# Linear attention merged with the third feed-forward part: another order of the steps inside a pass

## The reference, cut to what matters

```
x = x + _L2_xattn_ref(_layernorm(x, axis=-1), ctx_4096, ctx_4096)
x = x + _L2_ffn_ref(_layernorm(x, axis=-1), L2_ffn_router_w, L2_ffn_A, L2_ffn_B)
x = x + _L3_xattn_ref(_layernorm(x, axis=-1), ...)
```

## The kernel before

| step | engine, line | pass t works on |
|---|---|---|
| y transpose (y_tr) | PE L923, psY | t-3 |
| kv product | PE L913, psSO<-arena,kT | t-1 |
| e transpose (e_tr) | PE L929 | t |
| LN5 transpose, LN6 transpose | PE L614, psQ (or psTP) | t-4; e-2 |
| gate product | PE L628, psSO<-wkv,hT | e |
| out product | PE L951 to L953, psTP | t-2 |
| hidden transpose | PE L856 | e |
| expert product | PE L869, psKV | e |
| x add | DVE L1898 | t-3 |
| kvs | DVE L1901, L1904 (k_sb) | t-1 |
| statistics | DVE L1537 to L1539 | t-3 |
| eT low half | DVE L1515 kT | t |
| gates | DVE L1611 to L1572, with one exponential on ACT, L1142 | e |
| y | DVE L1917, L1919 (prob) | t-2 |
| LN5, LN6 low half (`ln_lo`) | DVE L1515 hT | t-4; e-2 |
| hidden low half | DVE L1515 oT | e |
| expert add | DVE L1838 | e-1 |
| maximum for k's softmax (ctx_max) | DVE L1878 | t+2 |
| q exponential, q copy (q_hi) | ACT L1394, L1108 qT | t-1 |
| ln_hi | ACT L1108 hT | t-4; e-2 |
| normalisation (`ln_norm_act`) | ACT L1373, xn | t-3; e-1 |
| kvs_lo, q_lo, rstd, nmr | POOL L573, L580, L451, L563 | |

## Time and profile before

### The profile page before, as it was taken

One profiled execution on the slowest core, in us unless ns is written; L12 is line 12 of the kernel. 1 busy time (PEld: TensorE's weight loads), 2 busy tenths in 40 slices (PEclk: granted clock), 3 DMA queues, 4 the chain that ended last, 5 costly groups with the idle time before them and its releaser, 6 DMA issues.

```text
span 1657.8 us, 27915 instructions
## 1 busy us (share of the span) xinstructions
PE 1544.3 (93%) x9690; PEld 1345.1 (81%) x9690; DVE 1064.4 (64%) x2585; ACT 820.7 (50%) x2869; POOL 336.9 (20%) x353
## 2 busy tenths in 40 slices
PE   6999999999999989889999999999999997767988
PEld 5898999999999978778888888888888776655766
DVE  6566556655655687756666666666666876754664
ACT  4556445554545553355555555555555414425540
POOL 4102101110101021222222223122222213313110
PEclk9999999999999999999999999999999997868989
DMA  5101010100001001101010101010100001100001
GB/s 199 31 26 57 9 51 27 39 27 26 26 27 39 27 28 48 39 26 39 26 39 26 39 26 43 22 64 24 42 30 4 30 4 51 61 1 20 33 4 51
DMA packets 13710, 59.43 MB, mean 36 GB/s; under 512 B 2131, under 2 KB 3155, under 8 KB 8454
## 3 DMA queue, kind: packets, MB, share of 16 engines
q1 hardware_dynamic: 13574, 57.67, 9.9%
HBM read 55.57 MB, written 2.10 MB: 35 GB/s over the span
## 4 chain that ended last, share of the span: by engine, by line
PE 51%; issue 29%; DVE 11%; POOL 4%; ACT 3%; DMA 1%; POOLq 0%; SPq 0%; ACTq 0%; DVEq 0%
PE psY L772 12%; PE psQ L697 8%; PE psKV L717 7%; PE psSO L760 2%; PE psSO L666 2%; PE psQ L682 2%; POOL wo L438 2%; PE psQ L1044 1%; PE psTP L682 1%; DVE wq L1515 1%; PE psSO L667 1%; PE psTP L727 1%; PE psKV L1006 1%; PE psKV L641 1%; PE psTP L745 1%
## 5 line engine op out<-in xcount | busy, mean ns | idle before, releaser
L772 PE MATMUL psY<-wo,oT 128*128 128x512 f32 x1536 | 384.7, 399 | 1.9 <-DVE oT L1515 1.3
L772 PEld LDWEIGHTS psY<-wo,oT 128*128 128x128 f32 x1536 | 278.4, 188 | 66.0 <-POOL wo L438 2.3
L697 PE MATMUL psQ<-wq,hT 128*128 128x512 f32 x768 | 212.2, 414 | 0.3 <-DVE wq L1515 0.3
L438 POOL TENSOR_TENSOR wo<-stage_o,wo 128x512 fp32r<-128x512 f32 (+2 forms) x72 | 93.7, 1331 | 322.9 <-ACT wo L1108 322.9
L697 PEld LDWEIGHTS psQ<-wq,hT 128*128 128x128 f32 x768 | 137.9, 193 | 24.6 <-DVE wq L1515 1.2
L539 POOL TENSOR_TENSOR rms<-ms_eps,minus_half 128x5 f32<-128x5 f32 x64 | 74.7, 1167 | 390.8 <-DVE ms_eps L1678 390.8
L1177 ACT ACTIVATE prob<-s_sb,neg_mx 128x64 f32<-128x64 f32 x256 | 86.1, 337 | 110.0 <-DVE neg_mx L1665 110.0
L1180 ACT ACTIVATE prob<-wide,neg_mx 128x128 f32<-128x128 f32 x256 | 99.7, 391 | 73.7 <-DVE neg_mx L1665 73.6
L1108 ACT ACTIVATE pT<-psTP 128x512 fp32r<-128x512 f32 (+1 forms) x128 | 62.3, 486 | 131.1 <-PE psTP L745 131.1
L717 PEld LDWEIGHTS psKV<-wkv,arena 128*128 128x128 f32 x768 | 99.4, 190 | 19.8 <-DVE kT L1515 15.7
L1515 DVE TENSOR_TENSOR pT<-psTP,pT 128x512 fp32r<-128x512 f32 (+1 forms) x128 | 70.7, 552 | 65.9 <-ACT pT L1108 65.3
(11 more groups left out here) (287 smaller groups left out, 3290.4 us busy)
## 6 DMA issues: line engine op xcount, KB each, us to landing
stage_q<-in_wq SPq DMA_DIRECT2D x16, 1024.0 KB, 5.3
stage_o<-in_wo SPq DMA_DIRECT2D x16, 1024.0 KB, 4.9
stage_kv<-in_wkv SPq DMA_DIRECT2D x12, 512.0 KB, 3.6
stage_q<-in_ctx SPq DMA_DIRECT2D x16, 256.0 KB, 4.2
stage_o<-in_ctxT SPq DMA_DIRECT2D x2, 1024.0 KB, 6.9
stage_q<-in_base SPq DMA_DIRECT2D x2, 1024.0 KB, 5.1
out<-x_res SPq DMA_DIRECT2D x8, 256.0 KB, 2.0
x_res<-in_x SPq DMA_DIRECT2D x1, 1536.0 KB, 13.2
```

Of the source, the lines that this page charges most:

```text
L438: g.tensor_tensor(dst[LO], stage, dst[HI].bitcast(f32), ALU.subtract).then_inc(ld[what + "_lo"], 1)
L697: m = mm(psQ[:], lat(xl, k, n), wq[:, wl, k, :], start=k == 0 and i == 0, stop=k == KT - 1 and i == 2)
L772: m = mm(psY[:], oT[:, ol, h, :], wo[:, wl, h, :], start=h == 0 and i == 0, stop=h == HQ - 1 and i == 2)
```

## The change

It moves steps inside `middle_step` on PE, ACT and DVE, and two inside POOL's loop. No instruction is dropped; the passes that run by themselves are 3 to 15 instead of 3 to 14, since ln_hi(6) and ln_lo(6) now handle tile e-3 at the start of a pass instead of tile e-2 at its end.

The new orders in a pass are these. PE: y transpose, kv product, e transpose, LN5 transpose, gate product, out product, hidden transpose, expert product, LN6 transpose. ACT: ln_hi(6), kvs_hi, eT_hi, q exponential, ln_hi(5), q copy, L1142, norm 5, context exponential, hidden_hi, norm 6. DVE: x add, LN6 low half, kvs, statistics, eT low half, (LN5 low half if e < 0), expert add, gates, y, LN5 low half, hidden low half, ctx_max. POOL: kvs_lo, rstd and nmr of norm 5, q_lo, rstd and nmr of norm 6.

The diff, cut to its core:

```diff
@@ gpsimd @@
-            if 0 <= e - 1 < NT:
-                ln_rstd(6, e - 1)
-                ln_nmr(6, e - 1, LNS[5]["xn"])
...
                 g.tensor_tensor(q_e[:, LO], q_sb[:], q_e[:, HI].bitcast(f32), ALU.subtract).then_inc(M["q_lo"], 1)
+            if 0 <= e - 1 < NT:
+                ln_rstd(6, e - 1)
+                ln_nmr(6, e - 1, LNS[5]["xn"])
@@ tensor, middle_step @@
-            if 0 <= e < NT:
-                gate_product(f, e)
+            if 0 <= t - 3 < NT:
+                u = t - 3
+                pe.wait_ge(s["y"], u + 1)
...
+                i.then_inc(s["y_tr"], 1)
             if 0 <= t - 1 < NT:
                 pe.wait_ge(s["eT_lo"], t)
...
-            if 0 <= e < NT:
-                pe.wait_ge(s["kvs"], min(t, NT))
-                hidden_transpose(f, e)
...
                 ln_transpose(5, t - 4, free)
+            if 0 <= e < NT:
+                gate_product(f, e)
...
             if 0 <= e < NT:
+                pe.wait_ge(s["kvs"], min(t, NT))
+                hidden_transpose(f, e)
                 experts(f, e)
...
-        for t in range(3, NT + 7):
+        for t in range(3, NT + 8):
             middle_step(t)
@@ scalar, middle_step @@
-            if 0 <= e < NT:
-                gate_exp(f, e)
+            if 0 <= e - 3 < NT:
+                ln_hi(6, e - 3)
...
-            if 0 <= e < NT:
-                hidden_hi(f, e)
...
+            if 0 <= t - 4 < NT:
+                ln_hi(5, t - 4)
             if 0 <= t - 1 < NT:
                 act.wait_ge(s["q_exp"], t)
                 need(act, s["out"], t - 1)
                 copy(q_e[:, HI], q_sb[:]).then_inc(s["q_hi"], 1)
-            if 0 <= t - 4 < NT:
-                ln_hi(5, t - 4)
+            if 0 <= e < NT:
+                gate_exp(f, e)
             if 0 <= t - 3 < NT:
                 ln_norm_act(5, t - 3)
-            if 0 <= e - 2 < NT:
-                ln_hi(6, e - 2)
+            if t + 1 < NT:
+                ctx_exp(t + 1)
+            if 0 <= e < NT:
+                hidden_hi(f, e)
             if 0 <= e - 1 < NT:
                 ln_norm_act(6, e - 1)
@@ vector, middle_step @@
-            if 0 <= e - 1 < NT:
-                experts_add(f, e - 1)
-            if 0 <= e < NT:
-                gates(f, e, e - 1 if e > 0 else None, 6)
...
+            if 0 <= e - 3 < NT:
+                ln_lo(6, e - 3)
...
+            if 0 <= t - 4 < NT and e < 0:
+                ln_lo(5, t - 4)
+            if 0 <= e - 1 < NT:
+                experts_add(f, e - 1)
             if 0 <= e < NT:
-                hidden_lo(f, e)
+                gates(f, e, e - 1 if e > 0 else None, 6)
...
+            if 0 <= t - 4 < NT and e >= 0:
+                ln_lo(5, t - 4)
+            if 0 <= e < NT:
+                hidden_lo(f, e)
...
-            if 0 <= t - 4 < NT:
-                ln_lo(5, t - 4)
-            if 0 <= e - 2 < NT:
-                ln_lo(6, e - 2)
```

More of the change, by code:

```diff
@@ L904, in middle_step @@
             s, f, e = M, FF[2], t - 5
-            if 0 <= e < NT:
-                gate_product(f, e)
+            if 0 <= t - 3 < NT:
+                u = t - 3
+                pe.wait_ge(s["y"], u + 1)
+                need(pe, s["x_add"], u)
+                if u == 0:
+                    pe.wait_ge(FS["x_add"], 2 * NT)
+                for c in range(KT):
+                    i = tr(psY[:, c * P:(c + 1) * P], y_T[:, c * P:(c + 1) * P], ident[:])
+                i.then_inc(s["y_tr"], 1)
             if 0 <= t - 1 < NT:
@@ L915, in middle_step @@
                 m.then_inc(s["kv"], 1)
[L916 to L924, removed]
             if t < NT:
@@ L1395, in middle_step @@
                                      scale=rstd[:, t - 1:t]).then_inc(s["q_exp"], 1)
-            if t + 1 < NT:
-                ctx_exp(t + 1)
+            if 0 <= t - 4 < NT:
+                ln_hi(5, t - 4)
             if 0 <= t - 1 < NT:
@@ L1889, in middle_step @@
                 link(V.memset(logits[:, f.E:8], -3e38))
-            if 0 <= e - 1 < NT:
-                experts_add(f, e - 1)
-            if 0 <= e < NT:
-                gates(f, e, e - 1 if e > 0 else None, 6)
-            elif e == NT:
-                stats_after(f, 6, NT - 1)
             if 0 <= t - 3 < NT:
@@ L1911, in middle_step @@
                 sub_hi(eT[:, LO], slices(psE), eT[:, HI]).then_inc(s["eT_lo"], 1)
+            if 0 <= t - 4 < NT and e < 0:
+                ln_lo(5, t - 4)
+            if 0 <= e - 1 < NT:
+                experts_add(f, e - 1)
             if 0 <= e < NT:
-                hidden_lo(f, e)
+                gates(f, e, e - 1 if e > 0 else None, 6)
+            elif e == NT:
+                stats_after(f, 6, NT - 1)
             if 0 <= t - 2 < NT:
```

## The result

The changed kernel takes 1684.77 us in the median of four runs (1683.02 to 1688.79), the kernel before beside it 1657.85 us. The ratio is 1.0165, with a 95% interval of 1.0138 to 1.0191, so it is slower by 23 to 32 us. Forecast were 1670 us and a range up to 1679: the sign is right, the size is not.

The account below looks back on a forecast made before the run. PE and DVE taking turns was held to bound the kernel. Terms summed to +1.8 us at full clock or +17.2 with a fall each pass; +14 was taken on the 1656.28 us median, giving 1670 us, range 1656 to 1679.

Parts of the forecast that it names:

- mechanism A: Favoured case: TensorE's clock falls in most passes, +14 us, between +8 and +22; chance 0.62.
- The loop of PE and DVE in turn: Passes 5 to 8: PE and DVE take turns; a full-clock pass takes 11.2 us against 9.9 before.
- The wait of norm 6: Passes 9 to 11: LN5 transpose waits for norm 6's low half, 1.5 us or more ahead of the gate product.
- The end of the phase: From pass 12's expert product to the following attention's first K product: 1.7 us later in all.
- The clock: TensorE's clock, the unknown term: new 4 us gap may halve it, making the sum +17.2 us instead of +1.8.
- the time of the gates: DVE's gates: exponential behind the q copy, hidden values done at 7.9 us into the pass instead of 7.6.
- The POOL order costs nothing: POOL's norm 6 step after the q low half is covered by later work; uncovered it would cost 0.5 to 1.3 us.
- the sum at half clock: Pass lengths added with a clock fall in each pass: last expert product ends at 1503.5 us, 15.5 later than before.
- E: Rival: clock stays at half for all of passes 5 to 12, +33 us; chance 0.05.
- B: Rival: clock holds at 2.4 GHz, +2 us; chance 0.13.
- C: Rival: faster, with DVE left as the only bound, -8 us; chance 0.13.
- D: Rival: semaphores, not queue order, set the same loop, 0 us; chance 0.07.

Follow-up runs that it names:

- e3: Changed kernel plus TensorE products that nobody reads, placed in its gaps, every order kept: phase 130.7 us against 147.4, whole 1.0044 of the kernel before.
- e1: Changed kernel with ScalarE's gate exponential moved ahead of the q copy: phase 143.5 us against 147.4, whole 1.0120 of the kernel before.
- e5: e1 plus POOL's q low half held until the hidden values are written: phase 139.5 us, whole 1.0097 of the kernel before.
- e2: Changed kernel with norm 6's high and low halves back at the end of a pass: phase 142.5 us against 147.4, whole 1.0093 of the kernel before.
- e4: Changed kernel with VectorE's hidden low half ahead of y and the LN5 low half: phase 144.2 us against 147.4, whole 1.0098 of the kernel before.

## Why the prediction was right, and where it was not

The direction and most of the mechanism were right, the size was not: 27 us longer, where 14 stood and at most 22 for mechanism A.

**The loop of PE and DVE in turn** held. PE's order, both gaps, and the L1141 row behind the qT row are as laid out. The lengths, 11.2 us for a pass at full clock (e3 has 11.3) and 13.8 with a fall (the changed kernel has 13.7), agree in part by luck: the 11.2 and 13.8 hold an LN6 transpose of 0.4 or 0.8 us, which the measured stretches from expert product 5 to 7 don't have, and gates of 2.9 us, where 3.6 (e3) and 3.75 were measured.

**The wait of norm 6** held: 1.47, 1.47 and 2.27 us in passes 9 to 11, where "1.5 us or more" stood. **The end of the phase** was forecast 1.7 us longer; from the last expert product to K's first product it is 15.1 us after and 13.5 before, 1.7 more by the unrounded rows (15.14 and 13.47).

**The clock** held as mechanism: it falls in the gaps, and e3 shows 16.5 us hanging on it, near the distance of the two ends of the sum (1.8 and 17.2). The step from 17.2 down to 14, "less some passes in which the clock comes back sooner", was a guess in the wrong direction: it fell in every one of passes 5 to 8. Over passes 5 to 12 the granted clock was 0.69, as forecast under 0.75.

**The step that failed is the time of the gates.** The text put the exponential behind the q copy at 0.3 us a pass (hidden done at 7.9 instead of 7.6), 1.2 us in four passes. Measured from the start of L1610 to the end of L1571 the gates of passes 5 to 8 take 4.9, 3.75, 3.7 and 3.7 us and not 2.9, so 4.5 us over the layout, and taking the cause away gave 6.4 us (e1, e5) and not 1.2. Two things were missing. The out product's result sets off a chain of two, the q copy and then POOL's q low half, and this second one, though moved in no line of the diff, now ran beside the gates: 0.7 us in each of passes 6 to 8, and in pass 5 L1577 (0.98) met it and L1585 (1.18) POOL's weight halves (L438) behind it. And DVE's wait for the exponential is longer with the fall: 0.5 us in passes 6 to 8, where e3, at full clock, has the 0.3 of the layout in passes 6 and 7; in pass 5, where no expert add holds DVE up, it is 1.2 in both. "The POOL order costs nothing" looked at when POOL would be ready, and not at what it would disturb.

By the end of the last expert product the sum at half clock had 15.5 us and the trace has 22.3. The missing 6.8 us, pass by pass (each from its y transpose to the next):

| | sum | measured | more |
|---|---|---|---|
| passes 0 to 4 | 28.9 | 29.7 | 0.8 |
| pass 5 | 13.2 | 14.5 | 1.3 |
| pass 6 | 12.2 | 13.7 | 1.5 |
| pass 7 | 13.8 | 14.6 | 0.8 |
| pass 8 | 13.3 | 13.7 | 0.4 |
| pass 9 | 12.3 | 13.3 | 1.0 |
| passes 10 to 12 | 31.8 | 32.8 | 1.0 |

Passes 5 to 8 are 4.0 us over, about the 4.5 of the gates. The 1.0 of pass 9 is a slip: the prediction's own layout gave 13.3 for it at half clock, and the sum was added up with 12.3. In pass 6 the sum had only 0.2 us for the fall (12.2 against 12.0), without a reason given. What is over before pass 5 and in passes 10 to 12 (to the end of the last expert product) stays open.

**The range.** The best guess lay 3 us under the sum for the worst clock, and the upper end 5.5 us over that sum. Between A, which ended at +22, and E, at +33, no mechanism was priced, and the measured +27 fell there.

**The rivals.** B (clock holds, +2) fell by the granted clock. C (faster by DVE alone) fell: DVE is busy 82.8 us of 147.4. D fell: the queue order decides, as moving norm 6's halves (e2) or one low half (e4) puts the whole under the changed kernel's interval. E fell, since the clock came back ahead of gate products 6 to 8: they take 1.66 to 1.67 us and not 2.91.

## What to carry to other kernels

In a loop that passes from engine to engine, a step that is "ready" is not free: ask of each queue what now stands between a result and its user, and follow each moved wait to the second follower, which may be on an engine that the diff hardly touches. When a gap on TensorE grows, price the products behind it at half clock too; if the gap can't be closed, products that nobody reads cost less here than the clock did. A small VectorE instruction on the critical chain should not run beside a wide one of GpSimd that reads the same memory. And before two kernels are compared by a stretch of one execution each, look at how much of that stretch is the same code, and how far it varies: here by 2.2 us, as much as some of the effects.

## What the hardware showed that was not expected

A VectorE instruction on 128x4 elements (L1577) took 0.98 us instead of 0.27 while the 1.27 us q low half of GpSimd ran. Another (L1585) took 1.10 to 1.11 instead of 0.22 beside it in e1, and 1.18 beside GpSimd's weight halves in pass 5 of the changed kernel; holding the q low half back by a wait brought all sixteen to their short time. Two others on one element per partition (L1581 and L1582) ran beside the same GpSimd instruction and kept their 0.15 and 0.17 us.

The kernel before had such a meeting too, of wide instructions. VectorE's two weight halves of pass 5 stand beside GpSimd's there, and alone in the changed kernel, and took 3.21 us before and 1.27 after:

```profile
1416.03 3.21 DVE L1515 TENSOR_TENSOR wq<-stage_o,wq 128x512 fp32r<-128x512 f32 x2
```

```profile
1423.77 1.27 DVE L1514 TENSOR_TENSOR wq<-stage_o,wq 128x512 fp32r<-128x512 f32 x2
```

And 102 added products, 3.1 us more of busy PE in the phase (89.8 to 92.9), made the phase 16.8 us shorter.
